# Delta attention written out block by block: one block's layer norm and projection interleaved with the next block's heads

## The reference

```python
q = silu(dwconv_causal(x @ Wq, qconv_w, qconv_b))      # 4 taps; the same for k and v
a = sigmoid(x @ Wa + ba);  beta = sigmoid(x @ Wb + bb)
def step(S, t):                                        # S: (B, H, 128, 128)
    y = einsum('bhvk,bhk->bhv', S, k_t)                # k scaled by 128 ** -0.5
    S = a_t[..., None] * S - (b_t[..., None] * (y - v_t))[..., None] * k_t[:, :, None, :]
    o = einsum('bhvk,bhk->bhv', S, q_t)
o = (o - mean(o)) * rsqrt(var(o) + 1e-5) * ln_g + ln_b # over the 128 of a head
out = (o * sigmoid(x @ Wg)) @ Wo                       # added to x
```

## Time and profile before

| | us |
|---|---|
| median of 3 runs | 3228.74 (3227.89 to 3228.85) |
| the profiled execution, its own time | 3217.28 |
| its span | 3215.6 |
| PE busy | 2511.6 (78%) |
| DVE busy | 1756.8 (55%) |
| POOL busy | 1283.7 (40%) |
| ACT busy | 1207.4 (38%) |

### The profile page before, as it was taken

The page is one execution under the profiler, slowest core; times in us unless marked ns, Lnnn a source line. Parts: engine busy times, 40 slices in busy tenths (PEclk is TensorE's granted clock), DMA queues, the critical chain, the costliest instruction groups (busy, mean ns, idle before and its releaser), DMA issues. The chain is left out here.

```text
span 3215.6 us, 45391 instructions
## 1 busy us (share of the span) xinstructions
PE 2511.6 (78%) x16906; PEld 2063.6 (64%) x16906; DVE 1756.8 (55%) x3327; ACT 1207.4 (38%) x2647; POOL 1283.7 (40%) x967
## 2 busy tenths in 40 slices
PE   6699846999896979776578848786578848759798
PEld 4688725888573758665566747675566737626677
DVE  2422365223455543476684696676684686645533
ACT  2333232332331423354443633464343633313233
POOL 0454313553201005427680496317670496210054
PEclk9799977999897979887768957797768957779899
DMA  0210002100000014043231332133231332010050
GB/s 30 79 59 20 0 17 79 49 30 0 17 1 18 1 46 150 14 105 96 92 105 45 125 104 87 41 109 110 76 105 51 119 125 74 33 48 1 35 161 13
DMA packets 121576, 198.86 MB, mean 62 GB/s; under 512 B 60048, under 2 KB 94752, under 8 KB 116256
## 3 DMA queue, kind: packets, MB, share of 16 engines
q1 hardware_dynamic: 121376, 196.21, 19.1%
HBM read 192.38 MB, written 3.81 MB: 61 GB/s over the span
## 5 line engine op out<-in xcount | busy, mean ns | idle before, releaser
L444 PE MATMUL PS<-XP_moe,WP_moe 128*128 128x512 f32 x1536 | 355.9, 393 | 30.3 <-POOL WP_moe L518 28.6
L444 PEld LDWEIGHTS PS<-XP_moe,WP_moe 128*128 128x128 f32 x1536 | 290.0, 190 | 91.2 <-issue 28.7
L1732 PE MATMUL PS<-ident,XT 128*128 128x128 f32 x512 | 114.0, 404 | 244.6 <-DVE XT L2061 227.9
L2007 DVE SCALAR_TENSOR_TENSOR M_delta<-PS,CW_delta,M_delta 128x256 f32<-128x256 f32 x576 | 231.7, 476 | 64.5 <-ACT M_delta L1891 63.7
L1732 PEld LDWEIGHTS PS<-ident,XT 128*128 128x128 f32 x512 | 91.2, 209 | 264.7 <-DVE XT L2061 132.4
L558 DVE TENSOR_TENSOR HF_moe<-SG_moe,PS 128x512 f32<-128x512 f32 x128 | 87.9, 687 | 265.3 <-ACT SG_moe L495 265.3
L1654 POOL TENSOR_SCALAR KQ_delta<-KQ_delta 128x256 f32<-128x256 f32 x64 | 54.3, 849 | 433.8 <-ACT KQ_delta L1904 433.8
L1678 PE MATMUL PS<-XP_delta,M_delta 128*128 x768 | 196.1, 404 | 35.7 <-DMA M_delta<-in_L_attn_b_heads 35.4
L1019 ACT ACTIVATE PR_attn<-PS,NM_attn 128x256 f32<-128x256 f32 (+1 forms) x384 | 135.4, 420 | 224.7 <-DVE NM_attn L1079 224.7
L524 POOL TENSOR_TENSOR HP_moe<-HF_moe,HP_moe 128x512 fp32r<-128x512 f32 x128 | 163.6, 1292 | 138.2 <-ACT HP_moe L488 138.2
L1256 PE MATMUL PS<-XP_rffn,UW_rffn 128*128 128x512 f32 x816 | 194.8, 395 | 4.8 <-POOL UW_rffn L1212 4.6
(11 more groups left out here) (316 smaller groups left out, 5737.0 us busy)
## 6 DMA issues: line engine op xcount, KB each, us to landing
M_delta<-gram_delta SPq DMA_DIRECT2D x32, 2304.0 KB, 8.8
M_delta<-in_L_attn_b_heads SPq DMA_DIRECT2D x64, 512.0 KB, 3.5
W_moe<-in_L_ffn_w SPq DMA_DIRECT2D x48, 512.0 KB, 4.7
CB_rffn<-routes_rffn SPq DMA_DIRECT2D x20, 512.0 KB, 22.6
XN<-in_L_attn_b_outs SPq DMA_DIRECT2D x16, 512.0 KB, 3.6
F_delta<-in_L_attn_b_outs SPq DMA_DIRECT2D x4, 2048.0 KB, 8.1
W_rffn<-in_L_ffn_tiles SPq DMA_DIRECT2D x4, 1536.0 KB, 11.7
W_rffn<-in_L_ffn_tiles SPq DMA_DIRECT2D x2, 2304.0 KB, 26.0
```

What stands on the lines that cost most here:

```text
L444: last = nc.tensor.matmul(PS[:, 2 * (g % 2) + i, :], up_w(qw, r, i, k, m), XP[qx][:, k, n * NB:(n + 1) * NB], start=(k + step == 0), stop= ...
L1732: last = nc.tensor.transpose(PS[:, 6 + r % 2, i * P:(i + 1) * P], W[:, B * h:B * (h + 1), :], core.ident[:])
L2007: nc.vector.scalar_tensor_tensor(TMP[:, r, i], win(4 * r + i)[:, :, tau:tau + BT], CW[:, i, h, tau:tau + 1], TMP[:, r, i], ALU.mult, ALU.a ...
```

## The change

- The loop over blocks is written out in Python. There is one set of semaphores for all four blocks, whose counts go on from block to block (`base_of`), and no barrier or clearing between blocks.
- The last state update, the layer norm and the projection of block n - 1 are interleaved with the heads of block n on every engine (`heads_and_norm`). Eight pairs of heads meet eight groups. For the last block the norm runs without heads, and its last state update is left out.
- The heads use one set of PSUM banks, 1 to 4. The norm has single banks: 6 for centre, 5 for variance and spread, 0 and 7 for the projection.
- ACT copies each of the three windows from PSUM to a new RAW in SBUF, and makes the first taps of q and k; POOL makes that of v from RAW (`tap`). DVE's taps read RAW and TMP.
- Sqrt on ACT and the reciprocal on DVE become an addition on DVE (`shift`) and a power of -0.5 on POOL (`power`).
- WH moves to X, TMP to XT, RAW and YB to M, RT gets its own tile. The weights of the first two heads of a block wait for the last W of the block before.

The core of the diff:

```diff
-    WH = room(1)[:, 0:2048].rearrange("p (r i k n) -> p r i k n", r=2, i=4, k=KD)
-    TMP = room(1)[:, 2048:2048 + 6 * B * BT].rearrange("p (r i b t) -> p r i b t", r=2, i=3, b=B)
-    RT = room(0)[:, 0:BH * BT // P]
+    WH = flat3(X[:]).rearrange("p (r i k n) -> p r i k n", r=2, i=4, k=KD)
+    TMP = flat3(XT[:])[:, 0:6 * B * BT].rearrange("p (r i b t) -> p r i b t", r=2, i=3, b=B)
+    RAW = room(0)[:, 0:6 * B * WIN].rearrange("p (r i b t) -> p r i b t", r=2, i=3, b=B)
+    YB = room(1)[:, 0:2 * D].rearrange("p (i d) -> p i d", i=2)
...
+        @block.gpsimd
...
+            def tap(n, h):
+                r, z = h % 2, base_of(n)
+                if h < 2 and n:
+                    pool.wait_ge(wt_mm, z["wt_mm"])
+                pool.wait_ge(ev_d, z["ev_d"] + 3 * h + 3)
+                if h >= 2:
+                    pool.wait_ge(act_d, z["act_d"] + 3 * (h - 2) + 3)
+                nc.gpsimd.tensor_scalar(TMP[:, r, 2], RAW[:, r, 2, :, TAPS - 1:], CW[:, 2, h, TAPS - 1:TAPS],
+                                        CB[:, 2, h:h + 1], ALU.mult, ALU.add).then_inc(tap_v, 1)
+            def power(n, g):
+                pool.wait_ge(var_d, n * NW + g + 1)
+                at = slice(g * NB // P, (g + 1) * NB // P)
+                nc.gpsimd.tensor_tensor(RT[:, at], RT[:, at], LN[:, 2:3].broadcast_to([P, NB // P]), ALU.pow).then_inc(root_d, 1)
+            def heads_and_norm(n):
+                if n:
+                    power(n - 1, 0)
+                for k in range(1, H // 2 + 1):
+                    if n < NBLK:
+                        tap(n, 2 * k - 2)
+                        if k > 1:
+                            scale_key(n, 2 * k - 3)
+                        tap(n, 2 * k - 1)
+                    if n and k < NW:
+                        power(n - 1, k)
+                    if n < NBLK:
+                        scale_key(n, 2 * k - 2)
...
+        @block.tensor
+        def _(pe):
+            def head(n, h):
+                r, z = h % 2, base_of(n)
+                pe.wait_ge(wh_in[r], 16 * (H // 2 * n + h // 2 + 1))
+                if h == 0 and n:
+                    pe.wait_ge(sadd_d, z["sadd_d"])
+                for i in range(4):
+                    if h:
+                        if i < 3:
+                            pe.wait_ge(ev_d, z["ev_d"] + 3 * (h - 1) + i + 1)
+                        else:
+                            pe.wait_ge(raw_d, z["raw_d"] + h)
...
+            def heads_and_norm(n):
+                if n:
+                    if n < NBLK:
+                        update(n - 1, NO - 1, 0)
+                    centre(n - 1, 0)
+                    if n < NBLK:
+                        update(n - 1, NO - 1, 1)
+                    variance(n - 1, 0)
+                    if n < NBLK:
+                        update(n - 1, NO - 1, 2)
+                        update(n - 1, NO - 1, 3)
+                    spread(n - 1, 0)
+                for k in range(1, H // 2 + 1):
+                    if n and k < NW:
+                        centre(n - 1, k)
+                    if n < NBLK:
+                        head(n, 2 * k - 2)
+                    if n:
+                        project(n - 1, 2 * k - 2)
+                        project(n - 1, 2 * k - 1)
+                    if n and k < NW:
+                        variance(n - 1, k)
+                    if n < NBLK:
+                        head(n, 2 * k - 1)
+                    if n and k < NW:
+                        spread(n - 1, k)
...
+        @block.scalar
+        def _(act):
+            def evacuate(n, h):
+                r, z = h % 2, base_of(n)
+                for i in range(3):
+                    act.wait_ge(p_mm, z["p_mm"] + 4 * h + i + 1)
+                    if h >= 2:
+                        act.wait_ge(conv_d, z["conv_d"] + 3 * (h - 2) + i + 1)
+                    if i < 2:
+                        if h >= 2:
+                            act.wait_ge(act_d, z["act_d"] + 3 * (h - 2) + i + 1)
+                        nc.scalar.activation(TMP[:, r, i], PS[:, 1 + i, 0:B * WIN].rearrange("p (b t) -> p b t", b=B)[:, :, TAPS - 1:],
+                                             bias=CB[:, i, h:h + 1], scale=CW[:, i, h, TAPS - 1:TAPS]).then_inc(tap0, 1)
+                    nc.scalar.copy(RAW[:, r, i].rearrange("p b t -> p (b t)"), PS[:, 1 + i, 0:B * WIN]).then_inc(ev_d, 1)
+            def heads_and_norm(n):
+                if n:
+                    square(n - 1, 0)
+                for k in range(1, H // 2 + 1):
+                    if n < NBLK:
+                        evacuate(n, 2 * k - 2)
+                        if k > 1:
+                            silus(n, 2 * k - 3)
+                    if n and k < NW:
+                        square(n - 1, k)
+                    if n < NBLK:
+                        evacuate(n, 2 * k - 1)
+                        silus(n, 2 * k - 2)
...
+        @block.vector
...
+                        nc.vector.scalar_tensor_tensor(TMP[:, r, i], RAW[:, r, i, :, tau:tau + BT],
+                                                       CW[:, i, h, tau:tau + 1], TMP[:, r, i], ALU.mult,
+                                                       ALU.add).then_inc(conv_d if tau == TAPS - 2 else tap_c, 1)
...
+            def heads_and_norm(n):
+                if n:
+                    if n < NBLK:
+                        dve.wait_ge(sdec_d, n * NO)
+                        add_update(n - 1, NO - 1, 0)
+                        add_update(n - 1, NO - 1, 1)
+                    shift(n - 1, 0)
+                    if n < NBLK:
+                        add_update(n - 1, NO - 1, 2)
+                        add_update(n - 1, NO - 1, 3)
+                for k in range(1, H // 2 + 1):
+                    if n:
+                        gated(n - 1, k - 1)
+                    if n < NBLK:
+                        taps(n, 2 * k - 2)
+                    if n and k < NW:
+                        shift(n - 1, k)
+                    if n < NBLK:
+                        taps(n, 2 * k - 1)
...
-    with nc.Fori(0, NBLK) as n:
-        one_block(n)
```

More of the change, by code:

```diff
@@ L1514, in delta_attention @@
     nc.all_engine_barrier()
[L1516 to L1532, removed]
-        rests = lambda o, jj: (NI - 1) * o + jj
-        with nc.Block() as block:
-            @block.sync
-            def _(sp):
-                outs = a["L1_attn_b_outs"]
@@ L1538, in _, with heads @@
+    chain_v, chain_p = s.sem("chain_v"), s.sem("chain_p")
+    wh_in = [s.sem("wh_in0"), s.sem("wh_in1")]
+    m_in = [s.sem("m_in0"), s.sem("m_in1")]
+    sc_out = [s.sem(f"sc_out{j}") for j in range(NC)]
+    by_b = lambda t: t.rearrange("p (h b) w -> p b h w", b=B)
+    rests = lambda o, jj: (NI - 1) * o + jj
+    with nc.Block() as block:
+        @block.sync
+        def _(sp):
+            outs = a["L1_attn_b_outs"]
+            def heads(n):
+                z = base_of(n)
                 for h in range(H):
@@ new lines, in rest @@
+            def rest(n, o, jj):
+                z = base_of(n)
+                ci = o * NI + jj
+                pe.wait_ge(base_d, z["base_d"] + ci)
+                for h in range(H):
+                    if h % 4 == 0:
+                        pe.wait_ge(wt_d, z["wt_d"] + NR * (ci - 1) + h // 4 + 1)
+                    for b in range(B):
+                        rows = slice(OC * b, OC * b + jj * C)
+                        last = nc.tensor.matmul(
+                            PS[:, 1 + b, h * 2 * C:(h + 1) * 2 * C].rearrange("p (q t) -> p q t", q=2),
+                            WT(o)[rows, h, :],
+                            GR[rows, o, h].rearrange("p (q t) -> p q t", q=2)[:, :, jj * C:(jj + 1) * C],
+                            start=True, stop=True)
+                last.then_inc(rest_mm, 1)
@@ new lines, in update @@
+            def update(n, o, r):
+                z = base_of(n)
+                pe.wait_ge(wt_d, z["wt_d"] + NR * (NI * (o + 1) - 1) + r + 1)
+                if r == 0:
+                    pe.wait_ge(base_d, z["base_d"] + NI * (o + 1))
+                else:
+                    pe.wait_ge(sadd_d, z["sadd_d"] + NR * o + r)
+                for i in range(4):
+                    h = 4 * r + i
+                    for b in range(B):
+                        rows = slice(OC * b, OC * (b + 1))
+                        last = nc.tensor.matmul(PS[:, 1 + b, i * P:(i + 1) * P], WT(o)[rows, h, :], KR(o)[rows, h, :],
+                                                start=True, stop=True)
+                last.then_inc(up_mm, 1)
@@ new lines, in gate @@
+            def gate(n, h):
+                z = base_of(n)
+                pe.wait_ge(wg_in, z["wg_in"] + 16 * (h // 4 + 1))
+                if h >= 2:
+                    pe.wait_ge(gate_d, z["gate_d"] + h - 1)
+                for k in range(KD):
+                    last = nc.tensor.matmul(PS[:, 6 + h % 2, 0:B * BT], WG[:, h % 4, k * P:(k + 1) * P],
+                                            XP[:, k, :, n * BT + TAPS - 1:n * BT + WIN],
```

(2 more changed lines are left out.)

899 lines of the change are left out of this document (432 added, 467 removed).

## The result

The changed kernel takes 3215.6 us (median of 10 runs, 3209.4 to 3221.7) beside 3227.2 for the kernel before (10 runs, 3218.5 to 3240.4). The ratio is 0.9963, with a 95% interval of 0.9948 to 0.9978: 0.37% faster, where 3252 us and slower had been forecast. The profiled execution of the changed kernel took 3215.73 us (span 3214.0).

A forecast was written before the change was run, and what follows sets the result against it. PE was taken to bound only part of the time, with PE, DVE and pace nearly level in the heads. +17.5 - 2.4 + 8 = +23 on 3217.28 gave 3240; with the median 11.5 higher, 3252 us, range 3208 to 3285.

The forecast's parts named there:

- port term: Block 0's heads: DVE's two-SBUF taps collide with POOL, 1.3 us a head, +17.5 us (0 to +23.6).
- the full stop: Block 0's heads: DVE taps stand through both POOL operations, upper bound 1.7 us a head, +23.6 us.
- the boundaries: Norm merged with next heads: 125.8 against 126.6 us, three times, -2.4 us in all (bounds -11 to +19).
- term of the chunks: Chunks after each block's heads, costed at nothing: 0 us change.
- the longer instruction stream: Unrolled program: if it starved an engine, that time would come on top; no size given.
- Rows 7: Trace rows cited for collisions: DVE's two-SBUF product took 5.04 us, not 2.53; POOL's product 7.39, not 5.06.
- Rival 2: Block 0's heads: ports do not collide with a tensor_scalar, +1 us there, 3235 us in all; chance 0.14.
- The pair: Merged blocks: two heads with one norm group take 13.4 us, 11.57 of it PE work (12.9 to 14.3).
- both waits: In each pair PE waits 0.5 us for ACT's square before variance, 1.1 for POOL's power before spread.
- its clock loss: First boundary, before the first head: PE still at its lower clock, 1.5 us added.
- The last norm: Last block's norm without heads: 6.35 us a group where it was 4.37, +8 us (2 to 27).
- the clock: Last norm: PE perhaps not granted 2.4 GHz; +27 in all at half clock, partly taken to reach +8.

The follow-up runs named there:

- e5: Kernel before, loop kept, plus 48 always-met waits on PE in every pass between last head and first gram: 3214.9 us in one run.
- e10: Kernel before, loop kept, plus 96 always-met waits on PE in every pass ahead of the first gram: 3224.2 us in one run.
- e11: The kernel of e5 again, timed in rounds against the kernel before: ratio 0.9948, 3216.7 us.
- e12: e8 plus 48 always-met waits ahead of block 0's first gram: ratio 0.9792 to the kernel before, 3161.4 us.
- e7: Changed kernel with POOL's pow replaced by a product with zero, so output is wrong: 3194.8 us, ratio 0.9880 to the kernel before.
- e6: Changed kernel with POOL's key scale written as a product of two tensors: 3215.4 us, ratio 0.9947 to the kernel before.
- stopped loops: Three profiled kernels with loop and PE stop: the kernel before, its unedited repeat (3230.8 us), and it with 16 always-met waits per pass (3231.5 us).
- e4: Changed kernel with v's first tap made by ACT, no tap on POOL: 3190.1 us, ratio 0.9871 to the kernel before.
- e3: Changed kernel with POOL's power ahead of the odd head's tap: 3190.6 us, ratio 0.9868 to the kernel before.
- e8: e3 plus ACT's square ahead of the silus and, in the last norm, PE's variance ahead of the projections: 3168.7 us, ratio 0.9800.
- e2: Kernel before with its block loop written out, barriers, clearing and order kept: 3213.3 us, ratio 0.9936 to the kernel before.

## Why the prediction was wrong

**Two steps failed, and the sign needed both.** The larger is the port term, "I take 1.3, nearer to the full stop", so +17.5 us for block 0's heads: the runs show +3.8. The other is the term of the chunks, "Costed at nothing": the runs show -8.6. With the first alone put right the sum is +9.4 us, with both +0.8, and the boundaries, 6.5 better than forecast, carry it below zero.

**"Costed at nothing: ... the chunks ..., the constant registers in place of the loop's. If the longer instruction stream starved an engine, that would be on top."** It named the right thing with the wrong sign. The loop kernel was the one whose PE was starved, once a pass, and the row for it stood in the trace of before ("issue", 3.2 to 4.3 us in L1692). I had read the boundary, where the change was, and took the chunks for untouched. In the changed kernel the stop is missing in three blocks: 5 us each before the first copy, and 2 us of it given back between the first and the fourth (also in e5, e10 and e11, whenever the stop is gone): -14.6 + 6.0 = -8.6 us. With the stop, POOL's next large product starts 0.3 us after the first copy, without it 4.6 to 4.7 us after; that this gives the 2 us back was not tested.

The stop hangs on the instructions ahead of it and not on the loop: e5 and e11 keep the loop and lose it, 16 more instructions move it, 48 more remove it. And the trace has what PE waits for. The page of the profile lists transfers of kind instruction during the run (before, then changed):

```profile
q8 instruction: 123, 2.02, 0.3%
```
```profile
q8 instruction: 115, 1.88, 0.2%
```

One of them (16 KB) lies in the stop that is shown above, between 1839.8 and 1843.1 in the kernel before:

```profile
q8 instruction: 1, 0.02, 1.7%
```

In the changed kernel's second gram of block 1, between 1840.83 and 1842.82, there is none:

```profile
q1 hardware_dynamic: 35, 0.65, 100.0%
```

(The view lists the queues that moved anything, and this is the only line.) The fourteen profiles have nineteen such stops in the second gram. In each of them exactly one transfer of this kind starts, 0.8 to 2.2 us after PE's last matmul, and PE goes on 1.3 to 1.5 us after the transfer's end; a twentieth stop, of 2.0 us in e12, goes on 1.4 us after one. Of the 37 second grams without a stop, 36 have no start of such a transfer in them, and one (e7, block 2) has one 0.2 us before its end. In e5's block 1 it starts at 1839.42, 3.2 us ahead of the gram. So PE stops because instructions have not arrived. Why they are asked for so late, and why 48 waits are enough to bring the transfer ahead, stays open.

**Block 0's heads, +17.5 (0 to +23.6).** Measured +3.8 (70.4 us against a mean of 66.6). The starts of block 0's Sigmoid, 1458.6 to 1461.4 in the kernels with the change but for e6, lie within those of the kernels without it only because block 0 began earlier in this profile: its first matmul is at 1388.2, against a mean of 1392.6 in the stopped loops. Over all profiles that start is at 1388.2 to 1392.3 in the seven kernels with the change and at 1389.6 to 1395.4 in the seven without. Most of this distance grows in the softmax attention ahead, which no edit touches (0.3 us between the two means at 800, 2.4 at 1100); its cause is open.

Rows 7 are right, and so is the collision; the step that failed is who pays. "nearer to the full stop" was taken from a DVE product that met one POOL operation of 5 us. Here DVE runs its taps one behind another and POOL's short operation has to find its way in: POOL's tap goes from 0.56 to 1.28 us, DVE's from 0.476 to 0.501, and POOL has time. What is left to pay is DVE's wait for POOL's tap (2.8 us in block 0), and e4, which has no such tap, has 3.3 of the 3.8 us back. Rival 2 (3235, "the ports do not collide") came nearest with +1, but for the wrong reason: a scale of 24.91 us in e4 is a collision.

The Trainium skill, SBUF — State Buffer, section SBUF: two separate sides, says that whichever of the two starts first has the shared ports for its whole instruction and that the other fully blocks. Rows 7 and the 5.32 us above agree. Block 0 agrees for POOL's side only: of the 138 DVE taps beside 30 POOL operations the longest took 0.655 us, so none stood through a POOL operation of 0.56 to 0.85, while in e4 one POOL operation stood through 25 us of DVE taps.

**The pair, 13.4.** Right, 13.6, with both waits at their places. Two terms inside were off and partly cancelled: pow 1.03 for 0.30 (inside the bound of 1.2), the tap 0.56 for 0.85 (below its lower bound). e3, e4, e7 and e8 take the waits away one by one and give 12.07, 12.07, 12.76 and 11.56.

**The three boundaries, -2.4.** -8.9 in the ledger. -5.4 of it is in e2 too, which only lacks the loop's end and jump, so the interleaving beyond that gives -3.5. Both lie within the forecast's bounds of -11 to +19 (by the pairs of 12.9 and 14.3 they should have read -13 to +17). The parts of the first boundary: 15.7 us to the first head (17.3 + 1.5 forecast with its clock loss), 102.9 for the heads (101.9), 4.3 to the table load (5.1).

**The last norm, +8.** +10.0 (62.1 against the mean of 52.1 of the stopped loops). The group was 6.84 for 6.35, because of pow (e7 is 0.81 shorter). Two thirds of the term had been put on the clock, and that part was too much: the granted clock of the stretch is 0.88, and a pair of projections takes 1.99 us in the groups from the second on, so these ran at the 2.4 GHz level with PE idle 2 us in each.

**The sum.** +3.8 for block 0, -8.9 at the boundaries, +10.0 for the last norm, and -8.6 for the chunks: -3.7. The earlier start of block 0 (-4.4) and the ledger's fourth-to-fifth line (-2.8, within its own spread) bring it to -10.9, beside -11.6 of the medians; neither of these two is shown to belong to the change. Of the miss of 36.4 us, 13.7 is the ports, 8.6 the stop, 6.5 the boundaries, -2 the last norm, 1.5 the median of before, which was 3227.2 in these runs, and 7.2 those two; 0.9 is left.

## What to carry to other kernels

Before costing a change, look in the profile for idle time of the busiest engine that has "issue" and no semaphore as its reason, in the whole program: a change that moves instructions can add or remove it, and it can be tried for nothing with some waits that are always met. When work of two stages is interleaved on an engine in order, write down for each hop of the inserted chain what stands ahead of it on every engine it passes; here three swaps of order (power before tap, square before silus, variance before projection) were worth 47 us by the medians, four times what the change itself gave. With two engines on one pair of ports, ask which of them has the free time, and put the price there; then look who waits for that engine, since a stream without gaps on the other can hold it for as long as the stream lasts.

## What the runs showed of the hardware

- PE stops for 2.9 to 4.3 us within a run of 256 instructions that wait for nothing: after 116 of its 128 matmuls in the loop kernels, 118 or 119 in block 0 of those written out, 112 with 16 more instructions ahead, and not at all with 48 and 96 more.
- In each of the nineteen stops of this kind one transfer of kind instruction starts (16 KB, 0.9 to 1.05 us), and PE goes on 1.3 to 1.5 us after its end.
- A POOL scale of 128x256 (0.85 us alone) took 24.91 us beside a gapless DVE stream of two-input SBUF operations, whose mean was 0.485 us (e4).
- POOL's pow of 128x4 takes 1.03 us (x32), a product of the same shape 0.20; with the product a pair was 0.84 us shorter.
- POOL's 128x256 operation of one tensor and two constants takes 0.56 us with DVE idle, and 1.28 beside a DVE stream of two-input SBUF operations, which itself slows by 5%.
- POOL's product of two tensors of 128x256, one of them a broadcast column, takes 0.83 us (mean of 64), no more than the scale by a constant (0.85).
